# First layer of a two-layer block: the squares of Z and Zq, their sums, roots and inverses taken in one set of wide instructions instead of two (blocks 4 to 31)

## The reference, cut to what matters

```python
Z1 = xk_c @ W + bb
mu = Z1.mean(-1, keepdims=True)
std = jnp.sqrt(Z1.var(-1, keepdims=True) + EPS)
x_hat = (Z1 - mu) / std
...
Wn, bn = (W - dW, bb - db)
Zq = xq_c @ Wn + bn
mu2 = Zq.mean(-1, keepdims=True)
std2 = jnp.sqrt(Zq.var(-1, keepdims=True) + EPS)
out = xq_c + g * ((Zq - mu2) / std2) + be
```

## Time and profile before

| | us |
|---|---|
| median of 3 runs (lowest, highest) | 926.8 (926.56, 928.77) |
| the profiled execution | 926.01 |
| its span, first to last instruction | 924.2 |
| busy in the span: PE, DVE, POOL, ACT | 861.4, 776.4, 638.0, 553.7 |
| mean granted TensorE clock | 0.985 of full speed |

### The profile page before, as it was taken

The page is one execution under the profiler, slowest core; times in us unless marked ns, Lnnn a source line. Parts: engine busy times, 40 slices in busy tenths (PEclk is TensorE's granted clock), DMA queues, the critical chain, the costliest instruction groups (busy, mean ns, idle before and its releaser), DMA issues.

```text
span 924.2 us, 19886 instructions
## 1 busy us (share of the span) xinstructions
PE 861.4 (93%) x7832; PEld 602.6 (65%) x7832; DVE 776.4 (84%) x1180; ACT 553.7 (60%) x845; POOL 638.0 (69%) x582
## 2 busy tenths in 40 slices
PE   2778999999997899999999999999999999999997
PEld 2566878788776797565576575565565665665564
DVE  7889999999997647978878979878979878879876
ACT  4546566766653555576576566576566666566663
POOL 5387788888883144786785876775876875776873
PEclk9799999999997999999999999999999999999999
DMA  8100000000000601010121120120120110120110
GB/s 216 50 2 2 2 2 3 2 2 4 3 2 1 182 2 41 40 67 22 46 67 33 49 79 21 46 66 24 59 78 22 46 67 23 60 78 21 46 53 24
DMA packets 25077, 38.29 MB, mean 41 GB/s; under 512 B 9444, under 2 KB 15608, under 8 KB 22936
## 3 DMA queue, kind: packets, MB, share of 16 engines
q1 hardware_dynamic: 23352, 34.74, 12.1%
q10 hardware_dynamic: 1632, 2.27, 0.8%
HBM read 28.29 MB, written 1.43 MB: 32 GB/s over the span
## 4 chain that ended last, share of the span: by engine, by line
PE 54%; DVE 24%; issue 12%; POOL 7%; ACT 3%; DMA 1%; SPq 0%; POOLq 0%; DVEq 0%
PE bank L1240 11%; PE bank L1242 10%; PE bank L1241 10%; DVE hdh L1034 6%; PE bank L1550 3%; PE quad L1582 3%; DVE add L1043 3%; PE bank L1406 2%; DVE mx L1027 2%; POOL arena L1151 2%; PE quad L1295 2%; POOL arena L1157 2%; PE bank L1601 1%; PE bank L1395 1%; PE quad L1378 1%
## 5 line engine op out<-in xcount | busy, mean ns | idle before, releaser
L1027 DVE TENSOR_REDUCE mx<-quad 128x4 f32<-128x2048 f32 x64 | 146.4, 2287 | 37.5 <-PE quad L1582 37.4
L1208 POOL CAST hdh<-xn 128x512 fp32r<-128x512 f32 x96 | 66.1, 689 | 155.1 <-ACT xn L662 155.1
L679 ACT ACTIVATE ex<-quad 128x2048 f32<-128x2048 f32 x64 | 120.6, 1884 | 59.0 <-PE quad L1592 59.0
L1210 POOL TENSOR_TENSOR hdl<-hd,hdh 128x512 fp32r<-128x512 f32 x96 | 129.6, 1350 | 7.7
L1210 POOL TENSOR_TENSOR hdl<-xn,hdh 128x512 fp32r<-128x512 f32 x96 | 128.9, 1343 | 7.7
L1240 PE MATMUL bank<-hdh,W2h 128*128 128x512 f32 x256 | 113.8, 445 | 6.1 <-DVE hdl L1037 5.4
L662 ACT ACTIVATE xn<-bank,b1c 128x512 f32<-128x512 f32 x128 | 87.8, 686 | 26.8 <-POOL hdl L1210 19.2
L662 ACT ACTIVATE hd<-bank,b1c 128x512 f32<-128x512 f32 x112 | 76.9, 687 | 44.7 <-PE bank L1242 29.1
L1241 PE MATMUL bank<-hdh,W2l 128*128 128x512 f32 x256 | 101.1, 395 | 0.0
L1242 PE MATMUL bank<-hdl,W2h 128*128 128x512 f32 x256 | 101.1, 395 | 0.0
L1240 PE MATMUL bank<-cH,W1h 128*128 128x512 f32 x192 | 81.0, 422 | 0.7 <-DVE cL L1054 0.7
(11 more groups left out here) (315 smaller groups left out, 2167.4 us busy)
## 6 DMA issues: line engine op xcount, KB each, us to landing
cwB<-gate_rows SPq DMA_DIRECT2D x16, 1024.0 KB, 4.7
kx<-kqh SPq DMA_DIRECT2D x32, 64.0 KB, 2.1
qx<-kqh SPq DMA_DIRECT2D x32, 64.0 KB, 2.1
W1r<-in_L_ffn_W SPq DMA_DIRECT2D x1, 1024.0 KB, 10.0
kx<-kql SPq DMA_DIRECT2D x16, 64.0 KB, 2.1
qx<-kql SPq DMA_DIRECT2D x16, 64.0 KB, 2.1
rec<-rec_rows SPq DMA_DIRECT2D x32, 32.0 KB, 2.2
out<-fin SPq DMA_DIRECT2D x4, 256.0 KB, 2.3
```

The source lines that it names most:

```text
L679: act.activation(ex[:, t % 2, :, :], quad[:, :, :], ACT.Exp, scale=float(AD) ** -0.5).then_inc(ROUND["exps_ready"], 1)
L1027: dve.tensor_reduce(mx[:, t, :, 0], quad[:, :, :], AX_X, ALU.max, negate=True).then_inc(ROUND["score_max"], 1)
L1208: pool.tensor_copy(hdh[:, m % RING, :], tile(n)).then_inc(ROUND["pool_split"], 1)
L1210: pool.tensor_tensor(hdl[:, m % RING, :], tile(n), hdh[:, m % RING, :], ALU.subtract).then_inc(ROUND["pool_split"], 1)
```

## The change

In iterations 4 to 31 (`BOTH`) one ACT instruction squares all 1024 columns, one DVE reduction makes the 16 sums, one root and one reciprocal of 16 columns follow. `squares_q`, `sum_squares_q`, `deviation_q` and `rdev_q` issue nothing in these iterations and work only in 32 to 35. `normed` waits for the common reciprocal. The places of the remaining instructions in each engine's order are the same. The statistics of both move into one tile `rz` of 16 columns a row (0 to 7 for Z, 8 to 15 for Zq).

```diff
-        rq = sb("rq", [P, 4, 3, 8])
+        rz = sb("rz", [P, 4, 3, 16])
+        BOTH = range(4, 4 * NC)
+        cols_of = lambda s: slice(0, 8) if s < 4 else slice(0, 16) if s in BOTH else slice(8, 16)
...
             def squares(s):
                 if s in LIVE:
                     act.wait_ge(CHUNK["z_ready"], s + 1)
-                    if s >= 4:
+                    if s in BOTH:
                         act.wait_ge(CHUNK["zq_ready"], s - 3)
-                    act.activation(by_pair(sqz[:, :]), z_of, ACT.Square).then_inc(CHUNK["z_squared"], 1)
+                        act.activation(piece(4, 1024).rearrange("p (a h c) -> p a h c", a=8, h=2), quad[:, 2:4, :].rearrange("p h (a c) -> p a h c", a=8),
+                                       ACT.Square).then_inc(CHUNK["z_squared"], 1)
+                    else:
+                        act.activation(by_pair(sqz[:, :]), z_of, ACT.Square).then_inc(CHUNK["z_squared"], 1)
...
-                    act.activation(sm[:, s % 4, 1, :], sm[:, s % 4, 0, :], ACT.Sqrt, bias=C("ttt_eps"), scale=1.0 / HD).then_inc(CHUNK["z_dev"], 1)
+                    act.activation(rz[:, s % 4, 1, cols_of(s)], rz[:, s % 4, 0, cols_of(s)], ACT.Sqrt, bias=C("ttt_eps"), scale=1.0 / HD).then_inc(CHUNK["z_dev"], 1)
...
             def squares_q(s):
-                if s in AFTER:
+                if s in AFTER and s not in BOTH:
...
             def deviation_q(s):
-                if s in AFTER:
+                if s in AFTER and s not in BOTH:
...
             def sum_squares(s):
                 if s in LIVE:
                     dve.wait_ge(CHUNK["z_squared"], s + 1)
-                    dve.tensor_reduce(sm[:, s % 4, 0, :], g3(sqz[:, :]), AX_X, ALU.add).then_inc(CHUNK["z_sumsq"], 1)
+                    src = piece(4, 1024).rearrange("p (h c) -> p h c", h=16) if s in BOTH else g3(sqz[:, :])
+                    dve.tensor_reduce(rz[:, s % 4, 0, cols_of(s)], src, AX_X, ALU.add).then_inc(CHUNK["z_sumsq"], 1)
...
-                    dve.reciprocal(sm[:, u, 2, :], sm[:, u, 1, :]).then_inc(CHUNK["z_rdev"], 1)
+                    dve.reciprocal(rz[:, u, 2, cols_of(s)], rz[:, u, 1, cols_of(s)]).then_inc(CHUNK["z_rdev"], 1)
...
             def sum_squares_q(s):
-                if s in AFTER:
-                    dve.wait_ge(CHUNK["zq_squared"], s - 3)
-                    dve.tensor_reduce(rq[:, s % 4, 0, :], g3(sq2[:, :]), AX_X, ALU.add).then_inc(CHUNK["zq_sumsq"], 1)
+                if s in AFTER and s not in BOTH:
+                    dve.wait_ge(CHUNK["zq_squared"], s + 1 - 4 * NC)
+                    dve.tensor_reduce(rz[:, s % 4, 0, 8:16], g3(sq2[:, :]), AX_X, ALU.add).then_inc(CHUNK["zq_sumsq"], 1)
 
             def rdev_q(s):
-                if s in AFTER:
-                    dve.wait_ge(CHUNK["zq_dev"], s - 3)
-                    dve.reciprocal(rq[:, s % 4, 2, :], rq[:, s % 4, 1, :]).then_inc(CHUNK["zq_rdev"], 1)
+                if s in AFTER and s not in BOTH:
+                    dve.wait_ge(CHUNK["zq_dev"], s + 1 - 4 * NC)
+                    dve.reciprocal(rz[:, s % 4, 2, 8:16], rz[:, s % 4, 1, 8:16]).then_inc(CHUNK["zq_rdev"], 1)
 
             def normed(s):
                 if s in AFTER:
-                    dve.wait_ge(CHUNK["zq_rdev"], s - 3)
-                    dve.tensor_tensor(by_pair(Am[:, s % 2, :]), zq_of, per_pair(rq[:, s % 4, 2, :]), ALU.mult).then_inc(CHUNK["normed_ready"], 1)
+                    if s in BOTH:
+                        dve.wait_ge(CHUNK["z_rdev"], s + 1)
+                    else:
+                        dve.wait_ge(CHUNK["zq_rdev"], s + 1 - 4 * NC)
+                    dve.tensor_tensor(by_pair(Am[:, s % 2, :]), zq_of, per_pair(rz[:, s % 4, 2, 8:16]), ALU.mult).then_inc(CHUNK["normed_ready"], 1)
```

More of the change, by code:

```diff
@@ L525, in deviation_q @@
             def deviation_q(s):
-                if s in AFTER:
-                    act.wait_ge(CHUNK["zq_sumsq"], s - 3)
-                    act.activation(rq[:, s % 4, 1, :], rq[:, s % 4, 0, :], ACT.Sqrt, bias=C("ttt_eps"), scale=1.0 / HD).then_inc(CHUNK["zq_dev"], 1)
+                if s in AFTER and s not in BOTH:
+                    act.wait_ge(CHUNK["zq_sumsq"], s + 1 - 4 * NC)
+                    act.activation(rz[:, s % 4, 1, cols_of(s)], rz[:, s % 4, 0, cols_of(s)], ACT.Sqrt, bias=C("ttt_eps"), scale=1.0 / HD).then_inc(CHUNK["zq_dev"], 1)
             def take_turned(s):
@@ L805, in xhat @@
                     dve.wait_ge(CHUNK["z_rdev"], s + 1)
-                    dve.tensor_tensor(by_pair(xh[:, u, :]), z_of, per_pair(sm[:, u, 2, :]), ALU.mult).then_inc(CHUNK["xhat_ready"], 1)
+                    dve.tensor_tensor(by_pair(xh[:, u, :]), z_of, per_pair(rz[:, u, 2, 0:8]), ALU.mult).then_inc(CHUNK["xhat_ready"], 1)
             def rate_of(s):
@@ L812, in rate_of @@
                     dve.wait_ge(CHUNK["z_rdev"], s + 1)
-                    dve.tensor_tensor(sm[:, u, 3, :], eta[:, s // 4, g, 8 * hf:8 * hf + 8], sm[:, u, 2, :], ALU.mult).then_inc(CHUNK["rate_ready"], 1)
+                    dve.tensor_tensor(sm[:, u, 3, :], eta[:, s // 4, g, 8 * hf:8 * hf + 8], rz[:, u, 2, 0:8], ALU.mult).then_inc(CHUNK["rate_ready"], 1)
             def gradient(s):
```

## The result

The changed kernel takes 938.47 us (median of 4 runs, 937.43 to 938.97), the kernel before beside it 927.05 (4 runs, 926.56 to 928.77). The ratio is 1.0118, with a 95% interval of 1.0101 to 1.0136: 11.4 us slower. Forecast were 935.3 us and a range of 930.5 to 941.0. The profiled execution took 938.28, its span is 936.5.

What follows compares the result with a forecast made beforehand. Order of time bounds the kernel: a DVE-POOL round trip of 7.01 us, with PE setting every fourth block. 5.0 + 3.5 + 0.4 = 8.9 us on 926.0 gave 934.9, stated as 935.3; range 930.5 to 941.0.

Steps and rivals of the forecast that it cites:

- The sum of the round trip: DVE's sum to the start of xhat: 1.20 + 0.37 + 0.22 = 1.79 us, +0.39 a block, bounds 0.32 to 0.49.
- Reciprocal to X stays at 0.22: From DVE's reciprocal to the start of xhat (L806): unchanged at 0.22 us though 16 columns wide.
- The square: ACT's 1024-column square: 1.04 us for 0.60, +0.44 where PE set the time, free where DVE sums late.
- The group: Four blocks, xhat's start in block 14 to block 18: 30.34 us for 29.09, +1.25, PE's path still setting it.
- rival A: Only the DVE-POOL round trip counts, PE catches up: groups of 29.6 us, total 931.7; chance 0.13.
- The second reciprocal: DVE's rdev_q removed: worth nothing where gradient waits for POOL, 0.22 us in each of blocks 5 to 7.
- rival B: ACT's later take_queries and take_keys delay PE, up to 0.5 us a block: 939 to 949 us; chance 0.09.
- rival E: ACT slower on the wide PSUM view; each 0.1 us costs only where the square is bare, 7 x 0.1; no chance given.
- The whole: All changed blocks, 4 to 31: 5.0 + 3.5 + 0.4 = 8.9 us slower.
- C: DVE's work sets the time, so work removed counts: 28 x 0.28 = 7.8 us faster, 919.0; chance 0.05.
- D: DVE's work sets the time but the root is bare: +0.17 us a block, 926.8 to 931; chance 0.08.
- its 1.34: DVE's pair of 512-column sums, if each waited for an emptied pipe: 1.34 us, merge saving 0.12, step +0.32; not adopted.

Runs made afterwards that it cites:

- e4: Changed kernel with the reciprocal split again into two of 8 columns in their old places; square, sum and root stay merged: 936.79 us, ratio 1.0095 to before.
- e6: Kernel before with DVE's two sums swapped in blocks 4 to 31, Zq's first, nothing merged: 939.81 us, ratio 1.0142.
- e2: Kernel before with only ACT's two squares merged into one of 1024 columns; sums, roots, reciprocals two by two: 929.67 us, ratio 1.0033.
- e11: Changed kernel with PE's bias products moved behind the query products in odd iterations from 5 on: 934.18 us, ratio 1.0075 to before.
- e9: Changed kernel plus an unused 8-column DVE reduction of one SBUF input in the wait for the root, blocks 4 to 31: 937.81 us, ratio 1.0121 to before.
- e10: Changed kernel plus an unused 8-column DVE product of two SBUF inputs in the wait for the root: 952.45 us, ratio 1.0282 to before.
- the sham: Kernel before with the statistics of Z and Zq kept in one 16-column tile, every instruction as narrow as before: 927.20 us, ratio 1.000.

## Why the prediction was right, and where its sizes were off

**The sum of the round trip.** Predicted 1.79 from sum to X and +0.39 a block, measured 1.87 and +0.46. The round trip was to take 7.40 and takes 7.47 to 7.49: +0.48 for the first step of a group and, since POOL's backlog goes, +0.34 for the next. The sum came out as taken (1.21, back to back). The root stood bare for 0.38 instead of 0.37, and the reciprocal to X is 0.29 instead of 0.22. The term that was mis-sized is "Reciprocal to X stays at 0.22": a reciprocal of 16 columns takes 0.25, one of 8 took 0.20 or less. e4 confirms it, 0.05 less a step with 8 columns; the other 0.02 is there with 8 columns too when the reciprocal comes out of a wait (0.24 to X in e4 and e6).

**The square.** Predicted 1.04, measured 1.03. It is bare only where PE comes last, as e2 shows. There the term was right for the changed kernel, 179.78 to the sum's start at 180.84 is 1.06, against 0.63 in the earlier trace rows.

**The group.** Predicted 30.34, measured 30.60 to 30.62. By the same sum with the measured step: two round trips +0.82, less POOL's 0.11 and PE's 0.05, is +0.66 for the bias; +0.43 for the square; sum to X 1.88 for 1.52, +0.36. That makes +1.45, and +1.5 was measured. The chain was right in each link: `bias` started 20.16 after X(14) where it had been 19.45, 0.71 later, and PE's run behind it took 7.52, before 7.49. e11 shows that this chain sets the group and not the round trip alone, as rival A would have it: four steps of 7.48 make 29.9, and the group was 30.6 until PE's wait was taken away.

**The second reciprocal, and what was costed at nothing.** Taken away, it was worth nothing in the usual block (e4), as predicted. The prediction gave it 0.22 in each of blocks 5 to 7, and this was wrong in its reason. The steps to X(5), X(6) and X(7) grew by 0.46, 0.19 and 0.27, together 0.92 where 0.6 was predicted. In the first and the third, `gradient` waited for POOL's `scaled`. In the second it came 3.19 after X(5) before, 2.92 in the changed kernel and 2.99 in e4, which has the reciprocal: so 0.07 is the reciprocal's. The other 0.20 is the router's scan between X(5) and `gradient`, 1.41 long before and 1.21 after; before, it had started 0.33 ahead of the end of POOL's `less`, and in the changed kernel `less` was over (the last section). ACT's `take_queries` came at 159.44 in iteration 15 and PE's `XK_` at 160.59: the cover held, so rival B fell. The wide view of PSUM costs ACT nothing that shows, 1.03 us against the 1.06 of the earlier trace rows, so rival E fell too.

**The whole.** 8.9 us predicted for blocks 4 to 31, 10.6 measured. 1.0 of the gap is in the four groups from X(14) on (6.0 for 5.0), 0.3 in blocks 5 to 7, 0.3 in X(10) to X(14) (+1.36 for +1.1), the rest in single blocks. The remaining 0.8 us between 10.6 and the medians' 11.4 are within the scatter of the runs. Each stretch came out dearer than forecast; only in the steps to X(6) and X(7) did a gain that nobody forecast stand in for the reciprocal's. Of the 3.4 us between the sum's 934.9 and the 938.28 of the profiled execution, 1.7 are in the blocks and 1.7 in stretches of which it said nothing.

**The rivals.** C and D gave DVE's work the lead. e6 gives the loss with equal work, e9 adds work at no cost: they fell. A fell by e11 and by groups of 30.6 where four round trips make 29.9. The Trainium skill's advice in "VectorE: DVE Perf Modes", section "Rules for kernel authors", to minimize the op count, pointed the wrong way: 112 instructions fewer took 11.4 us more. The Trainium skill, same page, section "The DRAIN you can't avoid", says that the next op waits for an empty pipe, and adds that one which is not held starts earlier; the prediction worked out its 1.34 from the first half alone. These rows agree with the second: e6's two sums start 0.59 apart and last 0.67 each.

## What to carry to other kernels

Before merging two narrow instructions, look at what lies between them. Here the second sum was the cover over the other engine's root, and the merge took the cover away for 0.06 us of saved reduction; swapping the two sums, with no merge, lost the same time. And ask which chain sets the end before counting instructions: an instruction fewer on an engine that waits anyway is worth nothing, one link longer in the loop is paid in every block. A wait is not free room for any instruction either: an 8-column product with two SBUF inputs put into it cost 15 us, a reduction with one input nothing.

## What the runs showed of the hardware that had not been expected

**DVE and POOL exclude each other for some instructions.** An 8-column product of two SBUF tensors lasted 1.23 us beside a POOL instruction of 1.28 us, a reduction of one SBUF tensor 0.15 us in the same place (e9, e10). DVE shows this as busy time and not as a wait. `xhat` and `normed`, with one input in PSUM and one in SBUF, lasted 0.68 to 0.69 us beside POOL too. The Trainium skill, "SBUF — State Buffer", section "🔬 SBUF: two separate sides", says that DVE with two SBUF inputs and a GpSimd instruction that reads SBUF share a pair of ports, held by whichever starts first for its whole length; e10 agrees.

The same reading fits rows that no experiment here tested by themselves, and in these both engines stand. `centre` (L838, two SBUF inputs) starts while POOL's `rated` (L1186) has 0.36 us to go and lasts 0.91; where it met no running instruction of POOL at its start it lasted 0.67 to 0.69 (95.11 and 111.56). POOL's `part` (L1172) starts while `centre` runs and lasts 1.49; in the one block where `centre` came behind it, it lasted 1.05, as long as `rated`, which has the same shapes. That would be 0.44 us of POOL in every block; what it costs the kernel is not shown.

```profile
95.11 0.67 DVE L838 SCALAR_TENSOR_TENSOR arena<-arena,sm 128x512 f32<-128x512 f32 x1
...
110.13 1.05 POOL L1172 TENSOR_TENSOR arena<-arena,sm 128x512 f32<-128x512 f32 x1
...
156.21 1.04 POOL L1186 TENSOR_TENSOR arena<-arena,sm 128x512 f32<-128x512 f32 x1
156.88 0.91 DVE L838 SCALAR_TENSOR_TENSOR arena<-arena,sm 128x512 f32<-128x512 f32 x1
157.21 1.49 POOL L1172 TENSOR_TENSOR arena<-arena,sm 128x512 f32<-128x512 f32 x1
```

The small rate product after `normed` lasts as long as `scaled` has left (0.47 to 0.87 us in the groups), where it harms nobody, since `gradient` waits for `scaled` too.

**The start of the kernel comes in two forms.** In the kernel before, PE's first products of 256 columns (from 20.25 us on) lasted 0.28 us and started 0.12 apart; in the changed kernel and in the sham they lasted 0.41 and started 0.21 apart, although the code there is the same, and the granted clock shown from 20 to 22 us is full in all of them. 0.41 is also what the same instructions last in the kernel before at 36.31, in a stretch whose granted clock is shown as 0.50, the lower of the two levels. Whether the first rows of the changed kernel ran at that level is not shown, and what decides between the two forms is open. Of the 13 profiles the seven with 0.28 had X(0) at 36.0 to 36.5 us and the mark ahead of block 4 at 68.85 to 69.28, the six with 0.41 had them at 37.0 to 38.3 and 69.71 to 70.75. First the changed kernel, then the kernel before:

```profile
21.78 0.41 PE L1249 MATMUL bank<-xth,wkh 128*128 128x256 f32 x1
```

```profile
36.31 0.41 PE L1241 MATMUL bank<-xth,wkl 128*128 128x256 f32 x1
```
